# 53 columns of the causal mask moved from mask products into constant rows of the score stacks

## The reference

```
attn = einsum('bhql,bkl->bhqk', q_lat, c_kv) / sqrt(hs)
attn = where(causal, attn, -inf);  attn = softmax(attn, axis=-1)
y    = einsum over the latent with v_eff        # then x = x + y * silu(experts(xn))
```

## Time and profile before

| what | value |
|---|---|
| time, median of 3 runs | 641.8 us (640.47 to 642.42) |
| time of the profiled execution | 642.34 us |
| its span, first to last instruction | 640.6 us |
| mean granted TensorE clock | 0.984 |
| PE busy | 601.3 us, 94% |
| DVE busy | 390.7 us, 61% |
| ACT busy | 363.0 us, 57% |
| POOL busy | 163.4 us, 26% |
| bytes moved by transfers | 35.60 MB |

### The profile page before, as it was taken

How to read it: one execution, slowest core, us unless ns; L and a number is a source line. 1 busy time by engine, 2 the same in 40 slices (tenths; PEclk the granted TensorE clock), 3 DMA queues, 4 the chain that set the end, 5 groups by cost and what they waited for, 6 DMA issues and landing times.

```text
span 640.6 us, 16904 instructions
## 1 busy us (share of the span) xinstructions
PE 601.3 (94%) x7002; PEld 382.2 (60%) x7002; DVE 390.7 (61%) x975; ACT 363.0 (57%) x743; POOL 163.4 (26%) x310
## 2 busy tenths in 40 slices
PE   7799999899999999999999999999999998997987
PEld 3345655576565766586566756586667665553564
DVE  3369676758668576848566675857675664413432
ACT  4331467755675575746674576646674667574420
POOL 4356122313223220332223230412232202210211
PEclk9899999999999999999999999999999999899888
DMA  3665003500341013310441014210430000100001
GB/s 85 162 157 135 9 1 99 141 9 4 87 121 56 4 35 99 92 41 9 107 110 42 2 52 112 62 41 11 124 92 27 3 10 1 42 1 1 4 2 33
DMA packets 28886, 35.60 MB, mean 56 GB/s; under 512 B 3947, under 2 KB 25258, under 8 KB 27658
## 3 DMA queue, kind: packets, MB, share of 16 engines
q1 hardware_dynamic: 28778, 34.52, 21.1%
q10 hardware_dynamic: 32, 0.01, 0.0%
HBM read 24.46 MB, written 9.96 MB: 54 GB/s over the span
## 4 chain that ended last, share of the span: by engine, by line
PE 60%; DVE 10%; issue 4%; ACT 4%; POOL 2%; DVEq 0%; POOLq 0%
PE ps_v L907 8%; PE ps_s L888 7%; PE ps_e L873 6%; PE ps_a L833 4%; PE ps_a L819 3%; PE ps_e L870 3%; DVE cand L1422 3%; PE ps_c L972 3%; PE ps_s L891 2%; PE ps_c L954 2%; PE ps_a L790 2%; PE ps_c L1057 2%; DVE stats L1344 1%; DVE hid L1406 1%; PE ps_c L941 1%
## 5 line engine op out<-in xcount | busy, mean ns | idle before, releaser
L1422 DVE TENSOR_REDUCE cand<-ps_s 128x4 f32<-128x512 f32 (+1 forms) x320 | 212.1, 684 | 63.7 <-PE ps_s L891 44.4
L1218 ACT ACTIVATE prob<-ps_e 128x512 f32<-128x512 f32 x320 | 188.8, 598 | 100.4 <-PE ps_e L873 96.4
L888 PE MATMUL ps_s<-kst,qst 72*128 72x128 bf16 (+1 forms) x1024 | 124.7, 233 | 8.9 <-DVE cand L1422 7.1
L873 PE MATMUL ps_e<-qst,kst 75*128 75x384 bf16 (+3 forms) x512 | 122.1, 300 | 0.0
L888 PEld LDWEIGHTS ps_s<-kst,qst 72*128 72x128 bf16 x1024 | 71.4, 98 | 69.3 <-DVE cand L1422 39.5
L907 PE MATMUL ps_v<-prob,vaug 128*32 128x512 f32 (+3 forms) x1024 | 89.5, 445 | 0.0
L870 PE MATMUL ps_e<-identb,negmask 128*128 128x256 bf16 (+1 forms) x320 | 81.0, 253 | 7.2 <-ACT prob L1218 7.0
L873 PEld LDWEIGHTS ps_e<-qst,kst 75*128 75x128 bf16 x512 | 50.3, 98 | 17.8 <-issue 0.3
L891 PE MATMUL ps_s<-negmask,identb 128*128 128x512 bf16 x128 | 48.8, 381 | 0.0
L706 PE MATMUL ps_e<-identb 128*128 128x512 bf16 x116 | 42.8, 427 | 3.1 <-POOL state L501 3.1
L870 PEld LDWEIGHTS ps_e<-identb,negmask 128*128 128x128 bf16 x320 | 31.3, 98 | 18.5 <-ACT prob L1218 14.4
(11 more groups left out here) (336 smaller groups left out, 922.7 us busy)
## 6 DMA issues: line engine op xcount, KB each, us to landing
qst<-q_scratch SPq DMA_DIRECT2D x48, 192.0 KB
kst<-k_scratch SPq DMA_DIRECT2D x16, 576.0 KB
q_scratch<-qparts SPq DMA_DIRECT2D x24, 128.0 KB, 2.3
k_scratch<-kparts SPq DMA_DIRECT2D x24, 128.0 KB, 2.3
x_res<-in_L_attn_x_dram SPq DMA_DIRECT2D x8, 256.0 KB, 2.8
xn<-in_L_attn_x_dram SPq DMA_DIRECT2D x7, 256.0 KB, 3.3
out_dram<-second SPq DMA_DIRECT2D x7, 256.0 KB, 2.5
max_scratch<-mrow SPq DMA_DIRECT2D x16, 96.0 KB, 1.7
```

The source lines that it names most:

```text
L873: last = mm(ps_e[:, bank, at:at + TOK - P * j], k[0:SROWS, hd, tok(j)], q[0:SROWS, hd, P * j:TOK], start=False, stop=True, skip_group_chec ...
L888: last = mm(ps_s[:, bank, w * n:w * (n + 1)], q[0:PAIRS, hd, tok(i)], k[0:PAIRS, hd, keys[0]:keys[1]], start=(n == 0), stop=True, skip_gro ...
L1218: af(prob[:, u, :], ps_e[:, u % 2, :], ACT.Exp).then_inc(S["e_emptied"], 1)
L1422: vec.tensor_reduce(cand[:, i, h0:h0 + FILLS * (len(hds) - 1) + 1:FILLS, S_SLOT[u]], ps_s[:, u % 2, :].rearrange("p (a c) -> p a c", a=len ...
```

## The change

Rows 75 to 127 of both stacks get constants (`MROWS` = 53 rows). In `qst` they hold the first 53 rows of the identity, once for each tile of 128 tokens, in `kst` the first 53 rows of `negmask`. A product over all 128 rows of a diagonal tile so adds the mask for its first 53 queries or columns, and the mask product only has to add the other 75 columns.

- `s_unit`: the four products of a diagonal unit run over 128 rows instead of 72. Rows 72 to 74 must add nothing there, so each `load_stacks` writes zeros into them in `qst` (`zeros_bf`, a fifth transfer). The mask product has 4 x 75 columns instead of 4 x 128.
- `e_unit`: the mask product has 75 or 2 x 75 columns instead of 128 or 2 x 128. The diagonal tile is a product of its own over 128 rows; what is right of it in the same bank is a second product over 75 rows, with its own weight load. Units 0 to 3 issue 3 products instead of 2, units 4 to 7 issue 4 instead of 3, units 8 and 9 issue 5 instead of 3.
- Start: POOL makes `negmask` and the two constant blocks (in the unused `prob` tile) before its layer norm work. SP copies them into the 16 heads of each stack, with transfers of 48 and 5 rows, plus the ones: for even sequences ahead of the loads of L410, for odd ones after the late loads. This is 1.79 MB for each parity (2 x 53 rows and 3 rows of 16 KB).
- TensorE waits for `pads_loaded0` and `pads_loaded1` before the first s unit of sequences 0 and 1; the wait for `ones_loaded` in `settle` is gone.

The core of the diff:

```diff
 QUAD = 32
-STACK_DMAS, WRITE_DMAS = 4, 6
+STACK_DMAS, WRITE_DMAS = 5, 6
 PAIRS = PARTS * PARTS * HD
...
 SROWS = PAIRS + PARTS
+MROWS = 128 - SROWS
+EVEN = 48
 HALF_HEADS = 8
...
         ones_bf = sb("ones_bf", [PARTS, TOK], BF16)
+        zeros_bf = sb("zeros_bf", [PARTS, TOK], BF16)
         nat = {n: sb("nat_" + n, s) for n, s in (
...
         prob = sb("prob", [P, UNITS, 512])
+        q_pad, k_pad = (prob[0:MROWS, 0, 256 * n:256 * n + 256].bitcast(BF16) for n in range(2))
         yT = sb("yT", [P, TOK])
...
         def _(sp):
+            def load_pads(p):
+
+                few = MROWS - EVEN
+                sp.wait_ge(S["pad_ready"], 2)
+                for st, pad in ((qst[p], q_pad), (kst[p], k_pad)):
+                    sp.dma_start(st[SROWS + few:P, :, :], bcast(pad[few:MROWS, :], 1, HEADS)).then_inc(S[f"pads_loaded{p}"], 16)
+                    sp.dma_start(st[SROWS:SROWS + few, :, :], bcast(pad[0:few, :], 1, HEADS)).then_inc(S[f"pads_loaded{p}"], 16)
+                sp.wait_ge(S["ones_ready"], 1)
+                sp.dma_start(kst[p][PAIRS:SROWS, :, :], bcast(ones_bf[:, :], 1, HEADS)).then_inc(S[f"pads_loaded{p}"], 16)
+
             sp.dma_start(xn[:, :, :], x_view[0]).then_inc(S["x_loaded"], 16)
...
             sp.dma_start(att[:, :, :], x_view[1]).then_inc(S["second_loaded"], 16)
+            load_pads(0)
             sp.wait_ge(S["small_zeroed"], 1)
...
                 sp.wait_ge(S["scratch_written"], 16 * b.count(WRITE_DMAS, WRITE_DMAS))
+                sp.wait_ge(S["zeros_ready"], 1)
                 q_rows = q_scratch[b.parity].rearrange("d r h q -> (d r) (h q)")[:, span]
...
                                  max_dma_last_dim=4096).then_inc(loaded, 16)
+                sp.dma_start(qst[b.parity][PAIRS:SROWS, heads, :], bcast(zeros_bf[:, :], 1, HALF_HEADS)).then_inc(loaded, 16)
                 sp.dma_start(kst[b.parity][0:PAIRS, heads, :].rearrange("p h q -> p (h q)"), bcast(k_rows, 1, PARTS)).then_inc(loaded, 16)
...
                     sp.dma_start(dst, src).then_inc(S["late_loaded"], 16)
-                sp.wait_ge(S["ones_ready"], 1)
-                for p in range(2):
-                    sp.dma_start(kst[p][PAIRS:SROWS, :, :], bcast(ones_bf[:, :], 1, HEADS)).then_inc(S["ones_loaded"], 16)
+                load_pads(1)
...
             g.memset(ones_bf[:, :], 1.0).then_inc(S["ones_ready"], 1)
+            g.memset(zeros_bf[:, :], 0.0).then_inc(S["zeros_ready"], 1)
+            chain(g.memset(negmask[:, :], 0.0))
+            chain(g.affine_select(out=negmask[:, :], in_=negmask[:, :], compare_op=ALU.is_ge, fill=NEG, base=0,
+                                  pattern=[[-1, P]], channel_multiplier=1))
+            for pad, of in ((q_pad, identb), (k_pad, negmask)):
+                g.tensor_copy(pad.rearrange("p (i c) -> p i c", c=P), bcast(of[0:MROWS, :], 1, NT)).then_inc(S["pad_ready"], 1)
             def constants():
-                chain(g.memset(negmask[:, :], 0.0))
-                chain(g.affine_select(out=negmask[:, :], in_=negmask[:, :], compare_op=ALU.is_ge, fill=NEG, base=0,
-                                      pattern=[[-1, P]], channel_multiplier=1))
                 for n, t in enumerate((wkT[:, 0:DS], wqT[:, 0:DS])):
...
                 pe.wait_ge(S["masks_ready"], 2)
-                pe.wait_ge(S["ones_loaded"], 32)
                 ready(PREP_OUT)
...
                 if u < 4:
-                    diag = ps_e[:, bank, 0:P].rearrange("p (a c) -> p a c", a=1)
+                    diag = ps_e[:, bank, MROWS:P].rearrange("p (a c) -> p a c", a=1)
                 else:
                     step = 384 if u < 8 else 256
-                    diag = ps_e[:, bank, :].rearrange("p (a c) -> p a c", c=P)[:, 0:step // P + 1:step // P, :]
-                mm(diag, negmask[:, :], bcast(identb[:, :], 1, len(todo)), start=True, stop=False, skip_group_check=True)
+                    diag = ps_e[:, bank, :].rearrange("p (a c) -> p a c", c=P)[:, 0:step // P + 1:step // P, MROWS:P]
+                mm(diag, negmask[:, :], bcast(identb[:, MROWS:P], 1, len(todo)), start=True, stop=False, skip_group_check=True)
                 for hh, j, at in todo:
                     hd = head_of(grp, hh)
-                    last = mm(ps_e[:, bank, at:at + TOK - P * j], k[0:SROWS, hd, tok(j)], q[0:SROWS, hd, P * j:TOK],
+                    last = mm(ps_e[:, bank, at:at + P], k[:, hd, tok(j)], q[:, hd, tok(j)],
                               start=False, stop=True, skip_group_check=True)
+                    if j < NT - 1:
+                        last = mm(ps_e[:, bank, at + P:at + TOK - P * j], k[0:SROWS, hd, tok(j)], q[0:SROWS, hd, P * (j + 1):TOK],
+                                  start=False, stop=True, skip_group_check=True)
                 last.then_inc(S["e_filled"], 1)
...
                 i, keys, hds = S_UNIT[u]
+                if b.c < 2 and grp == 0 and u == 0:
+                    pe.wait_ge(S[f"pads_loaded{b.parity}"], 80)
+                rows = P if u < NT else PAIRS
                 for n, hh in enumerate(hds):
...
                     hd = head_of(grp, hh)
-                    last = mm(ps_s[:, bank, w * n:w * (n + 1)], q[0:PAIRS, hd, tok(i)], k[0:PAIRS, hd, keys[0]:keys[1]],
+                    last = mm(ps_s[:, bank, w * n:w * (n + 1)], q[0:rows, hd, tok(i)], k[0:rows, hd, keys[0]:keys[1]],
                               start=(n == 0), stop=True, skip_group_check=True)
                 if u < NT:
-                    last = mm(ps_s[:, bank, :].rearrange("p (a c) -> p a c", a=GH), identb[:, :], bcast(negmask[:, :], 1, GH),
+                    last = mm(ps_s[:, bank, :].rearrange("p (a c) -> p a c", a=GH)[:, :, MROWS:P], identb[:, :],
+                              bcast(negmask[:, MROWS:P], 1, GH),
                               start=False, stop=True, skip_group_check=True)
```

More of the change, by code:

```diff
@@ L328, in two_layers @@
         k_scratch = nc.dram_tensor("k_scratch", (2, PARTS, HD, HEADS, TOK), BF16).ap()
-        names = """const_ready mask_step loaded ones_ready ones_loaded prep_pe prep_out prep_out2 prep_sign small_zeroed b2_ready
+        names = """pad_ready pads_loaded0 pads_loaded1 zeros_ready const_ready mask_step loaded ones_ready prep_pe prep_out prep_out2 prep_sign small_zeroed b2_ready
         q_loaded k_loaded cent_loaded route_loaded second_loaded late_loaded cent_ss_ready cent_rn_ready masks_ready
```

## The result

The changed kernel takes 651.28 us (median of 4 runs, 650.68 to 651.83), the kernel before in the same job 641.13 us (4 runs, 640.29 to 642.42). The ratio is 1.016 with a 95% interval of 1.014 to 1.018: **slower by some 10 us**, where 637.0 us was forecast.

The account below looks back on a forecast made before the run. PE was taken to set the time outside the first iteration (DVE there), with masks mostly on the path from 65 to 584 us. 642.34 - 9.6 (masks) + 4.8 (start) = 637.5, 637.0 us against the median; range 631.5 to 644.0.

Parts of the forecast that it names:

- The start, added: Head of the kernel: POOL's constants and SP's copies make the first e unit 4.8 us later, ends 1.5 and 8 us.
- 0.86 each and 4.3 us in all: SP's queue at the start: five added transfers priced from the ones transfer, two of which took 1.72 us.
- DVE is now 2.7 us later: Head: `loaded` complete at 19.7 us against DVE's preparation at 17.02, delaying the whole head and first iteration by 2.7 us.
- The second place: Transfer queue ahead of sequence 1's scratch writes: odd copies hold it 7.6 us, 3 hidden; first e unit 4.3 us later.
- POOL: Start: POOL's blocks, mask and copies complete `pad_ready` at about 6.2 us; its layer norm step's 1 us delay disappears.
- The masks: Shorter s and e mask products on TensorE save 9.6 us; a sequence's step falls from 70.8 to 69.3 to 69.6 us.
- One-tile masks: E mask with one tile, 128 to 75 columns: gain taken as 0, the next product's weight load (0.055 us) being later.
- The waits for DVE: S units' first loads wait for DVE's row maxima (39.5 us before); these waits should grow and take part of the gain.
- 12.3 to 9.6: The masks' gain on the path: upper end 12.3 us, 78% of it taken because part turns into waits for DVE and ACT.
- Odd start columns: Rival, chance 0.05: masks streaming from odd column 53 take twice the time a column, costing 6 us: 652.6 us.
- The start costs more than the masks give: Rival, chance 0.10: in SP's queue neither parity's 1.79 MB is hidden, first e unit 14.5 us late: 646.7 us.
- an idle queue: Held against the dear start: the transfer queue is idle for much of the first 20 us and again around 40.

Follow-up runs that it names:

- e3_late_odd: Changed kernel with the odd stacks' copies issued in sequence 1 behind its residual load, sequence 1 on the old products: 645.47 us, ratio 1.008 to the kernel before.
- e7_late_even_clean: Changed kernel, even copies behind sequence 0's residual load (old products, no zero transfers there), ones ahead of the early odd copies: 643.25 us, ratio 1.000 to before.
- the cleaned late form: Changed kernel with all constant copies late, sequences 0 and 1 on old products, POOL's new work behind its old: 634.06 us, ratio 0.985 to before.
- e1_start_only: All transfers, copies and waits of the changed kernel, but the products of the kernel before: 665.87 us, ratio 1.039 to the kernel before.
- e8_wide_source: Changed kernel with constant blocks four times as wide, so rows are copied in 4 KB pieces instead of 1 KB: 653.05 us, ratio 1.015 to before.

## Why the prediction was wrong

The step that failed is the second term of the sum, "The start, added": forecast 4.8 us, measured 21.2 us at the first exp (20.95 at the first e unit). At 16.4 us it is more than the whole error of 14.3. 641.8 - 9.6 + 21.2 is 653.4 us. That 2.2 us less behind the last exp bring this to 651.2, next to the 651.3 measured, is luck: they hang on where the clock was low, and no term of the sum had them.

- **"0.86 each and 4.3 us in all" failed.** I read two transfers of 48 KB as the price of ones of 768 KB, so priced issues, not bytes. The five took 10.4 us (6.01 to 16.41), the loads behind them 9.0 instead of 6.3, and the last issue ended at 25.4, not 16.7. 1.79 MB at 143 GB/s are 12.5 us. Had I divided by even the 185 GB/s of the earlier trace rows in this place, as the rival did, the loads would have moved by 9.7 us + 1.8.
- **"DVE is now 2.7 us later" failed with it.** The first expert product is 12.9 us late: 14.9 us of SP's delay less the 3.5 us that the forecast counted as slack, and 1.5 more. The clock of 0.50 from 18 to 38 us, behind a stop of 14.18 us, is the likely source of these 1.5 and of the 1.2 us that are added by the first row maximum. That was not varied.
- **The second place: right mechanism, size too small.** Counted were 7.6 us (1.79 MB at 228 GB/s are in fact 7.9) less 3 hidden and 3 more of slack at the first e unit; the odd copies cost 8.8 us (changed kernel against e3_late_odd) or 7.1 (e7_late_even_clean against before). The odd bytes at 143 GB/s alone are 12.5 us.
- **POOL was right**: `pad_ready` at 6.0 us (6.2 forecast), and e7_late_even_clean shows that its work delays nothing.
- **The masks were right**: 9.6 us forecast, 9.8 measured from the first exp to the last. A step shrank by 1.42 us, to 69.38 (69.3 to 69.6 forecast). L914 and two-tile L887 are as forecast, and the cleaned late form shows the gain by itself, 8.5 us with six sequences of eight on the new products.
- **One-tile masks were wrong**, with little effect: the next product starts after 0.03 to 0.04 us, not 0.055. I took the 0.055 us from the start of the load to its product for the price of the load. In the steady part before, the same pair has 0.053, and after the change, with the load unchanged, 0.032: it was the length of the 128 columns ahead. The row that I used came right out of a wait, which a steady step does not have. The rest of the term was a little too high in return: PE saved 17.9 us, not 19.
- **The waits for DVE hardly grew in the table of waits, but they did on the path.** The same two rows as in the earlier trace rows, 39.5 and 14.4 us before:

```profile
PEld ps_s L911 <- DVE cand L1446: 40.5, 85, 1.2
...
PEld ps_e L887 <- ACT prob L1242: 14.1, 19, 1.9
```

  In the chain of waits the row maxima have 4.7% of the 450 us up to the last exp (21.1 us), where they had 4.0% of 459 (18.4). These 2.7 us are what the forecast gave away (12.3 to 9.6), in the place that it named.

- **Odd start columns cost nothing**: 300 columns from column 53 take 0.13 us, 0.43 ns each, as the columns in the earlier trace rows.

The rival that came nearest was "The start costs more than the masks give": its place was right, its 14.5 us were too few, and 0.10 was too little for a term whose price no row of before showed. My range allowed half of it only. The arithmetic for it, bytes by rate with nothing hidden, stood in the forecast; what I held against it, an idle queue, does not help those who stand behind the bytes. What neither had is the clock: a stop of PE is paid once in waiting and again at 0.50 behind it, up to 5 us where the low clock fell on full work (e1_start_only).

**Open** stays why the copies go at 143 GB/s with full engines, where the stack loads go at 185 and are not full. In the traces a packet of 1024 bytes takes 0.115 us from SBUF and 0.14 from DRAM, one of 4096 bytes 0.41 from SBUF (e8_wide_source), and the stack loads' of 4096 bytes from DRAM take 0.29. So neither longer pieces alone nor DRAM alone gives the stack loads' rate; long pieces from DRAM were not tried, and the destination (53 rows from row 75 up) was not changed in any run. The transfers of 5 and 3 rows are not ruled out either.

## What to carry to other kernels

Price a transfer by its bytes at the rate of a full queue, and then go down the issuing queue and ask of each entry behind it who waits for it: at the start of this kernel, 1.8 MB cost 7 to 14 us in each place of the first 65 us where they were tried, and at most 0.4 us behind them. Then look at the granted clock behind each new stop. Constants that save a little in every pass need not be there for the first: let the first pass of each buffer work the old way, and load them where no product waits for what stands behind them. When a transfer is moved, each wait on its neighbours moves too; two of my runs measured that instead of their question.

## What the runs showed of the hardware

- A product of 75 columns with a new 128-column bf16 weight load behind it lets the next product start after 0.033 us (median of the steady part), 0.032 us behind the start of that load; between weight changes no 0.055 us are needed. The Trainium skill ("TensorE: Matmul & The Clock Gate", section "Weight-path perf modes") has a fast load at about twice the speed, as measured. This trace does not speak against it: if a plain load took a product's 0.43 ns a column, 128 columns would be 0.055 us and half of that 0.027 (an estimate), which fits into 0.032. How long a load takes by itself no run here shows.
- Of a parity's four copies out of SBUF the first took SP 0.64 to 0.75 us to issue, in all sixteen cases with pieces of 1 KB, the other three 0.8 to 7.0 us each, and the four together 6.9 to 11.8 us. Out of DRAM an issue took 0.30 to 0.43 us, and the loads behind blocked instead. A single row of 16 KB took 1.27 us. Bytes ahead alone do not block: in the earlier trace rows two issues took 0.86 us each with 1.0 MB of stack packets still to come.
- Copies into 53 rows ran at 139 to 143 GB/s from SBUF at a share of 1.08 to 1.16, with pieces of 1 KB; with pieces of 4 KB two stretches had 170 and 141. From DRAM it was 141, then 129 and 108 with the first loads among them. The stack loads of before moved 185 at 0.81.
- In both long stops of PE after the change (of 14.18 and 7.84 us) the granted clock fell to 0.50, at 18 and 83 us, and it stayed there while PE worked again. Between the first exps of sequences 0 and 1, where the work is nearly the same in all runs, 0 to 2.8 us at 0.50 go with 54.9 to 55.6 us, 4.6 with 55.9, 5.6 with 56.4, 9.1 with 58.7 and 11.8 with 60.7.
